# Edge groups of eight tiles in two slots, with sums and one-hot rows in two places

## The chip, the cores and the metric

One core of one Trainium2 chip. The time is the device time of one execution in microseconds; the kernel before has three of them, 4353.99, 4359.96 and 4360.02 us (median 4359.96).

## The reference, cut to what matters

The program is a chain of four graph layers over 3125 nodes with 128 features and 100000 edges that are sorted by destination. The change lies in the last layer, which sends a message along every edge:

```python
m_in = jnp.concatenate([h[src], h[dst], edge_attr], axis=1)
msg = jax.nn.relu(m_in @ msg_w1 + msg_b1) @ msg_w2 + msg_b2
agg = jax.ops.segment_sum(msg, dst, num_segments=h.shape[0])
```

## The kernel before, in words

Nodes are held in 25 blocks of 125 (`B`), edges in tiles of 128. Because matmul and sum commute, the edge stage computes only the relu and its sum by destination; `msg_w2` is applied in `update_phase`. `message_table_phase` has prepared two tables: h @ (the source half of `msg_w1`) in HBM (`dr.table`), and h @ (the destination half) plus bias in SBUF as three bf16 parts (`a3.q_parts`).

`edge_phase` (line 2019) takes the edges in groups of `GT` = 4 tiles, 196 groups in 49 rounds of `SLOTS` = 4 slots. For a group in slot s:

- SyncE (L2060, L2061) loads the destinations of its 512 edges, broadcast over 125 partitions (`dst_row`), and the edge attribute with its parts (`ea_row`).
- POOL (L2076) gathers the source rows by four indirect DMAs, one per tile, into `rows[s]`. It waits for `s_pre[s]`, that is for the identity matmul of the group that had the slot before (L2073).
- VectorE `turned` (L2102) compares `dst_row` with the lane numbers of a block: `hot_t[s]`, a one-hot matrix, 125 lanes by 512 edges.
- PE `inputs` puts the input of the relu together in one PSUM bank per slot: edge attribute (L2152, 4 matmuls), destination rows `hot_t` x `q_parts` (L2160, 12 matmuls, 3 for each tile), and the gathered rows by an identity matmul of 512 columns (L2167), which counts up `s_pre[s]`. An fp32 matmul shows as two rows of the trace, a bf16 one as one.
- ScalarE (L2204) applies relu to the bank's 512 columns and writes `act[s]`.
- VectorE `sums` first adds the sum of the visit before from its PSUM bank to `agg_t` (L2093), then makes `hot[s]` (L2111), one-hot rows with edges on partitions. PE `sums` (L2179) multiplies `act` and `hot`, 4 fp32 matmuls, into the one bank `SUMS`.

A group whose edges lie in more than one block is visited once for each block (`blocks.each`, L2009): the steps of L2102, L2160, L2093, L2111 and L2179 are repeated. The list of each group's first and last block, `g.groups`, is made in `setup_phase` (L300 to L314) from the smallest and largest destination of its tiles.

The order is written out by hand. PE and VectorE do `inputs` or `turned` of the next group, then `sums` of this one (`round_of`, L2185, L2118). POOL and SyncE run ahead, up to four groups, held by `s_pre` alone.

Of the kernel before, what the change touches and what calls it, by code (L numbers as in the profile page):

```python
# [16 lines left out]
B = 125  # L17
# [23 lines left out]
SLOTS = 4  # L41
# [83 lines left out]
def setup_phase(nc, g, io):  # L125

    with Phase(nc, "setup") as ph:
# [16 lines left out]
        NGR = NT // 4  # L144
# [94 lines left out]
        def _(v):  # L239
# [60 lines left out]
            for k, (i, op) in enumerate(((1, ALU.min), (0, ALU.max))):  # L300
                last = v.tensor_reduce(gm[:, k, :], mxb[0:1, i, :].rearrange("a (n t) -> a n t", t=4), AX.X, op)
# [445 lines left out]
def program(nc, io, out):  # L747
    ctx = ExitStack()
    Phase.used.clear()
    with ctx:  # L750
# [15 lines left out]
        g.groups = sb("groups", [1, NT // 4], I32)  # L766
# [1252 lines left out]
def edge_phase(nc, g, dr, a3):  # L2019
# [3 lines left out]
    GT = 4  # L2023
    W = GT * 128
    ROUNDS = (E // 128 + 1 + GT * SLOTS - 1) // (GT * SLOTS)
    with Phase(nc, "edge") as ph:
        rows = [ph.sb(f"rows{s}", [128, GT, D]) for s in range(SLOTS)]
        act = [ph.sb(f"act{s}", [128, GT, D]) for s in range(SLOTS)]
        hot = [ph.sb(f"hot{s}", [128, GT, B]) for s in range(SLOTS)]
# [4 lines left out]
        lane = ph.sb("lane", [128, 1])  # L2034
        ps = ph.ps()
        s_lane = ph.sem("lane")
        s_rows = [ph.sem(f"rows{s}") for s in range(SLOTS)]
# [11 lines left out]
        SUMS = SLOTS  # L2049

        @block.sync
        def _(sp):
            dst = dr.dst_rows.rearrange("(r s k) -> r s k", s=SLOTS, k=W)
            ea = dr.ea_rows.rearrange("i (r s k) -> i r s k", s=SLOTS, k=W)
            with sp.Fori(0, ROUNDS) as r:
                for s in range(SLOTS):

                    sp.wait_ge(s_pre[s], sp.snap(r + 1))
                    sp.sem_inc(s_tick, 1)
                    sp.dma_start(dst_row[s][:], dst[bass.ds(r, 1), s, :].to_broadcast([B, W])).then_inc(s_dst[s], 16)  # L2060
                    sp.dma_start(ea_row[s][:], ea[:, bass.ds(r, 1), s, :].rearrange("i a k -> i (a k)")  # L2061
                                 ).then_inc(s_ea[s], 16)

        @block.gpsimd
        def _(pool):
            pool.iota(lane_id[:], [[1, B]], base=0, channel_multiplier=0,
                      allow_small_or_imprecise_dtypes=True).then_inc(s_lane, 1)
            pool.iota(lane[:], [[0, 1]], base=0, channel_multiplier=1,
                      allow_small_or_imprecise_dtypes=True).then_inc(s_lane, 1)
            for r in range(ROUNDS):  # L2070
                for s in range(SLOTS):

                    pool.wait_ge(s_pre[s], r + 1)  # L2073
                    for i in range(GT):
                        t = (r * SLOTS + s) * GT + i
                        pool.indirect_dma_start(rows[s][:, i, :], None, dr.table,  # L2076
                                                bass.IndirectOffsetOnAxis(ap=g.src_idx[:, t:t + 1], axis=0)
                                                ).then_inc(s_rows[s], 16)

        @block.vector  # L2080
        def _(v):
# [5 lines left out]

            def add_sums(n):

                v.wait_ge(s_sum, n)  # L2090
                v.wait_ge(s_added, n)
                at = a3.agg_t[:, bass.ds(v.snap(before, min_val=0, max_val=NB - 1) * B, B)]
                v.tensor_tensor(at, at, ps[:, SUMS, 0:B], ALU.add).then_inc(s_added, 1)  # L2093

# [12 lines left out]
            def sums(r, s):  # L2107
                def one(d):
                    add_sums(added.next())
                    v.reg_mov(before, d)  # L2110
                    v.scalar_tensor_tensor(hot[s][:], bc(g.dst[:, bass.ds(r * (SLOTS * GT) + s * GT, GT)], B),  # L2111
                                           g.block_base[:, bass.ds(d, 1)],
                                           lane_id[:].unsqueeze(1).to_broadcast([128, GT, B]),
                                           ALU.add, ALU.is_equal).then_inc(s_hot, 1)

# [21 lines left out]
        def _(pe):  # L2137
# [3 lines left out]
            pe.sem_inc(s_sum, 1)  # L2141
            for s in range(SLOTS):
                pe.sem_inc(s_free[s], 1)
                pe.sem_inc(s_pre[s], 1)
                pe.sem_inc(s_act[s], 1)

            def inputs(r, s, ahead):

                pe.wait_ge(s_act[s], r + 1)
                pe.wait_ge(s_ea[s], r * 16 + 16)  # L2150
                for i in range(GT):
                    pe.matmul(ps[:, s, i * 128:(i + 1) * 128], ea_row[s][:, i * 128:(i + 1) * 128], a3.w_parts[:],  # L2152
                              start=i == 0, stop=False, skip_group_check=True)

                def one(d):
                    n = used[s].next()
                    pe.wait_ge(s_hot_t[s], n)
                    for i in range(GT):
                        for p in range(3):
                            last = pe.matmul(ps[:, s, i * 128:(i + 1) * 128], hot_t[s][:, i * 128:(i + 1) * 128],  # L2160
# [5 lines left out]
                pe.wait_ge(s_rows[s], r * (16 * GT) + 16 * GT)  # L2166
                pe.matmul(ps[:, s, :], g.ident[:], rows[s][:].rearrange("p a k -> p (a k)"), start=False, stop=True,  # L2167
                          skip_group_check=True).then_inc(s_pre[s], 1)

            def sums(r, s):  # L2170

                pe.wait_ge(s_act[s], r + 2)

                def one(d):
                    n = summed.next()

                    pe.wait_ge(s_hot, n)
# [14 lines left out]

            inputs(0, 0, False)
# [195 lines left out]
```

## Time and profile before

| what | value |
|---|---|
| median of three runs | 4359.96 us |
| the profiled execution: its own time | 4348.9 us |
| its span | 4347.1 us |
| PE busy | 3458.5 us, 80% |
| VectorE (DVE) busy | 1530.1 us, 35% |
| ScalarE (ACT) busy | 1228.8 us, 28% |
| POOL busy | 818.1 us, 19% |
| mean granted clock of PE over the span | 0.898 |

The span is the time from the first to the last instruction. A line of the timeline gives the start in us from the span's start, how long the instruction (or the merged run of instructions, with its count) takes, engine, line, operation, and in brackets how long the engine was idle before it and what ended that. "issue" means that the profile shows nothing that it waited for, "remote" that the semaphore moved at a time at which no row of its writer ends. Matmul ends are modelled. PEld are PE's weight loads. SPq are the DMAs that SyncE issues. A granted clock of 1.00 is 2.4 GHz, of 0.50 is 1.2 GHz.

### The profile page before, as it was taken

How to read it: one execution, taken by the hardware profiler on the slowest of the kernel's cores; microseconds unless marked ns; L12 is line 12 of the kernel's file. 1: busy time of each engine (PE TensorE's matmuls, PEld its weight loads, DVE VectorE, ACT ScalarE, POOL GpSimd, SP SyncE). 2: the span in 40 equal slices, each digit the busy share in tenths (PEclk: the TensorE clock that was granted, in tenths of full speed). 3: DMA queues.
4: the chain of work that ended last, by engine and by line, in shares of the span. 5: the costliest groups of instructions: out<-in, count | busy, mean ns of one | idle time of the engine just before them, and what ended most of it. 6: DMA issues, size and time to landing. Idle time of an engine off the chain costs nothing. (4 is left out here: it accounts for less than half of the span.)

```text
span 4347.1 us, 81151 instructions
## 1 busy us (share of the span) xinstructions
PE 3458.5 (80%) x23430; PEld 2425.0 (56%) x23431; DVE 1530.1 (35%) x4257; ACT 1228.8 (28%) x3843; POOL 818.1 (19%) x839
## 2 busy tenths in 40 slices
PE   2887778888988989897899999995665666666666
PEld 1334445566764444343799999994444444445454
DVE  8766556666760210002441111123222222222223
ACT  1455556677860210002432221212000000000000
POOL 3100000000000000000000000001666565656552
PEclk7999999999999999997999999997777777777777
DMA  2001111223349378993343222251222222222221
GB/s 58 0 29 44 58 58 58 87 88 102 102 134 237 92 184 188 204 210 88 80 124 88 74 80 73 67 145 35 66 65 64 60 64 57 63 61 63 59 59 40
DMA packets 120584, 381.40 MB, mean 88 GB/s; under 512 B 32903, under 2 KB 75262, under 8 KB 106556
## 3 DMA queue, kind: packets, MB, share of 16 engines
q1 hardware_dynamic: 95090, 326.87, 28.2%
q0 software_dynamic: 25216, 51.44, 5.4%
q8 instruction: 99, 1.62, 0.2%
q14 instruction: 179, 1.47, 0.1%
HBM read 294.59 MB, written 83.62 MB: 87 GB/s over the span
## 5 line engine op out<-in xcount | busy, mean ns | idle before, releaser
L2076 POOL DMA_INDIRECT edge_rows<-src_table,src_idx x784 | 759.5, 969 | 501.8 <-issue 195.3
L571 ACT ACTIVATE build_scaled<-build_lanes,w 128x128 f32<-128x128 bf16 x1132 | 440.2, 404 | 496.1 <-DVE build_lanes L529 468.9
L2179 PE MATMUL edge_ps<-edge_hot,edge_act 128*128 128x125 f32 x1760 | 305.9, 329 | 312.1 <-DVE edge_hot L2111 241.7
L2179 PEld LDWEIGHTS edge_ps<-edge_hot,edge_act 128*128 128x128 f32 x1760 | 288.6, 239 | 467.3 <-DVE edge_hot L2111 305.4
L529 DVE TENSOR_SCALAR build_lanes<-key_id,lane,one_w 128x128 f32<-128x128 f16 x1132 | 402.7, 356 | 382.3 <-PE build_ps L642 284.3
L642 PE MATMUL build_ps<-build_keys,build_scaled 128*128 128x300 bf16 (+1 forms) x2264 | 504.0, 305 | 29.0 <-ACT build_scaled L571 24.4
L634 PE MATMUL build_ps<-build_keys,build_lanes 128*128 128x300 bf16 (+1 forms) x1132 | 350.6, 310 | 170.3 <-DVE build_keys L531 149.2
L1041 PE MATMUL prop_ps<-prop_rows,y 125*128 125x500 f32 (+1 forms) x1050 | 413.6, 552 | 52.3 <-DMA prop_rows<-adj_rows 45.4
L2204 ACT ACTIVATE edge_act<-edge_ps 128x512 f32<-128x512 f32 x196 | 117.1, 597 | 1159.9 <-remote 654.7
L531 DVE TENSOR_SCALAR build_keys<-key_id,key,win_base 128x300 bf16<-128x300 f16 (+1 forms) x1132 | 423.7, 374 | 0.8
L1263 POOL TENSOR_SCALAR qk_half_b<-a_wob 125x128 f32<-125x128 f32 x1 | 2.1, 2061 | 1894.0 <-DMA a_wob<-L_gnn_Wo_b_dram 1894.0
L638 PE MATMUL build_ps<-build_keys,build_lanes 128*128 128x300 bf16 (+1 forms) x1132 | 344.3, 304 | 0.0
L1041 PEld LDWEIGHTS prop_ps<-prop_rows,y 125*128 125x128 f32 x1050 | 190.1, 193 | 274.6 <-issue 199.3
L2160 PE MATMUL edge_ps<-m_q_parts,edge_hot_t 125*128 x2640 | 243.3, 255 | 124.8 <-DVE edge_hot_t L2102 67.9
L2093 DVE TENSOR_TENSOR m_agg_t<-m_agg_t,edge_ps 128x125 f32 x221 | 63.0, 285 | 729.8 <-remote 469.9
L634 PEld LDWEIGHTS build_ps<-build_keys,build_lanes 128*128 128x128 bf16 x1132 | 111.0, 98 | 345.9 <-DVE build_keys L531 321.0
L642 PEld LDWEIGHTS build_ps<-build_keys,build_scaled 128*128 128x128 bf16 x2264 | 188.5, 100 | 180.0 <-ACT build_scaled L571 87.5
L2160 PEld LDWEIGHTS edge_ps<-m_q_parts,edge_hot_t 125*128 125x128 bf16 x2640 | 194.8, 115 | 160.2 <-issue 145.4
L2167 PE MATMUL edge_ps<-edge_rows,ident 128*128 128x512 f32 x392 | 267.2, 769 | 5.6 <-issue 3.5
L1565 PE MATMUL orders_ps<-a_xp,n 125*125 125x256 bf16 (+2 forms) x3000 | 262.4, 249 | 0.0
L1565 PEld LDWEIGHTS orders_ps<-a_xp,n 125*125 125x125 bf16 x3000 | 258.9, 139 | 0.6 <-issue 0.4
L1565 PE MATMUL orders_ps<-a_xp,orders_panel 125*125 125x256 bf16 (+2 forms) x3000 | 259.0, 247 | 0.0
(386 smaller groups left out, 4331.0 us busy)
## 6 DMA issues: line engine op xcount, KB each, us to landing
prop_rows<-adj_rows SPq DMA_DIRECT2D x85, 1367.2 KB
cnt_panels<-build_cnt SPq DMA_DIRECT2D x50, 683.6 KB
adj_rows<-build_adj_t SPq DMA_DIRECT2D x25, 1367.2 KB
n<-cnt_panels SPq DMA_DIRECT2D x40, 683.6 KB
orders_panel<-cnt_panels SPq DMA_DIRECT2D x40, 683.6 KB
edge_dst_row<-dst_rows SPq DMA_DIRECT2D x196, 125.0 KB
h<-cnt_panels SPq DMA_DIRECT2D x20, 683.6 KB
prop_rows<-adj_rows SPq DMA_DIRECT2D x85, 158.7 KB
```

What stands on the lines that cost most here:

```text
L529: v.tensor_scalar(lanes[s][:], g.key_id[:, 0:128], g.lane[:, at], g.one_w3[:, at], ALU.is_equal, ALU.mult).then_inc(s_lanes[s], 1)
L531: v.tensor_scalar(keys[s][:, 0:KW[q] + q], g.key_id[:, 0:KW[q] + q], g.key[:, at], g.win_base[:, q, bass.ds(e, 1)], ALU.subtract, ALU.is_e ...
L571: a.activation(scaled[s][:], half(lanes[s], 1), ACT.Copy, scale=g.w12[:, bass.ds(t, 1)]).then_inc(s_scaled[s], 1)
L634: done = pe.matmul(ps[:, count_bank(j, parity), 0:KW[j % 2]], half(lanes[s], 1), keys[s][:, 0:KW[j % 2]], start=first, stop=False, skip_gr ...
L638: pe.matmul(ps[:, weight_bank(j), 0:KW[j % 2]], half(lanes[s], 0), keys[s][:, 0:KW[j % 2]], start=first, stop=False, skip_group_check=True)
L642: last = pe.matmul(ps[:, weight_bank(j), 0:KW[j % 2]], half(scaled[s], i), keys[s][:, 0:KW[j % 2]], start=False, stop=False, skip_group_ch ...
L1041: last = pe.matmul(ps[:, c, 0:n * B], (y[0:B] if h else g.h)[:, row, 0:D], rows[row % R][:, b0 * B:(b0 + n) * B], start=at == 0, stop=at = ...
L1565: last = pe.matmul(ps[0:B, bank, at.start:hi], panel[i][:, b * B:(b + 1) * B], x_in[k][:, b, p, at.start:hi], start=False, stop=b == NB - ...
L2076: pool.indirect_dma_start(rows[s][:, i, :], None, dr.table, bass.IndirectOffsetOnAxis(ap=g.src_idx[:, t:t + 1], axis=0)).then_inc(s_rows[s ...
L2160: last = pe.matmul(ps[:, s, i * 128:(i + 1) * 128], hot_t[s][:, i * 128:(i + 1) * 128], a3.q_parts[:, bass.ds(d, 1), p, :].rearrange("p a ...
L2167: pe.matmul(ps[:, s, :], g.ident[:], rows[s][:].rearrange("p a k -> p (a k)"), start=False, stop=True, skip_group_check=True).then_inc(s_p ...
L2179: last = pe.matmul(ps[:, SUMS, 0:B], act[s][:, i, :], hot[s][:, i, :], start=i == 0, stop=i == GT - 1)
```

## The change

Groups have eight tiles (`GT` = 8) and there are two slots: 98 groups in 49 rounds. `g.groups` and the reductions that make it have half the entries. A slot owns two PSUM banks, one for each half of four tiles (`bank`); the two banks of the sums are 4 and 5, taken in turn (`side`), and `hot` too has two places by parity. Identity matmul, relu and the wait of the gathers go by halves: `s_pre` and `s_act` count up twice per group, `s_rows` is one semaphore for each half. VectorE makes the hot rows of a visit before it adds the sum of the one before. PE waits for `s_added` ahead of a sum. PE also gets matmuls whose result nobody reads (`keep_on`): zeros of 512 columns into bank 7, three ahead of the gathered rows of each group and two ahead of its sums.

```diff
-SLOTS = 4
+SLOTS = 2
...
-        NGR = NT // 4
+        NGR = NT // 8
...
-    GT = 4
+    GT = 8
+    HT = GT // 2
...
-        hot = [ph.sb(f"hot{s}", [128, GT, B]) for s in range(SLOTS)]
+        hot = ph.sb("hot", [128, 2, GT * B])
...
+        still = ph.sb("still", [128, HT * 128], BF16)
...
-        SUMS = SLOTS
+        SUMS, IDLE = 2 * SLOTS, 7
+
+        def bank(s, i):
+
+            return ps[:, 2 * s + i // HT, i % HT * 128:(i % HT + 1) * 128]
+
+        def half_of(tile, i):
+            return tile[:, HT * i:HT * i + HT, :].rearrange("p a k -> p (a k)")
...
-                    sp.wait_ge(s_pre[s], sp.snap(r + 1))
+                    sp.wait_ge(s_pre[s], sp.snap(r * 2 + 1))
...
+            pool.memset(still[:], 0.0).then_inc(s_still, 1)
...
-
-                    pool.wait_ge(s_pre[s], r + 1)
                     for i in range(GT):
+                        if i % HT == 0:
+                            pool.wait_ge(s_pre[s], 2 * r + 1 + i // HT)
...
-                                                ).then_inc(s_rows[s], 16)
+                                                ).then_inc(s_rows[s][i // HT], 16)
...
+            def side(n):
+                return v.snap(n & 1, min_val=0, max_val=1)
+
             def add_sums(n):
 
-                v.wait_ge(s_sum, n)
+                v.wait_ge(s_sum, n + 1)
                 v.wait_ge(s_added, n)
...
             def sums(r, s):
                 def one(d):
-                    add_sums(added.next())
-                    v.reg_mov(before, d)
-                    v.scalar_tensor_tensor(hot[s][:], bc(g.dst[:, bass.ds(r * (SLOTS * GT) + s * GT, GT)], B),
+                    n = added.next()
+
+                    v.wait_ge(s_sum, n)
+                    v.scalar_tensor_tensor(hot[:, bass.ds(side(n), 1), :].rearrange("p a (t k) -> p (a t) k", k=B), bc(g.dst[:, bass.ds(r * (SLOTS * GT) + s * GT, GT)], B),
                                            g.block_base[:, bass.ds(d, 1)],
                                            lane_id[:].unsqueeze(1).to_broadcast([128, GT, B]),
                                            ALU.add, ALU.is_equal).then_inc(s_hot, 1)
+                    add_sums(n)
+                    v.reg_mov(before, d)
...
+            def keep_on(n):
+
+                for i in range(n):
+                    pe.matmul(ps[:, IDLE, :], still[:, 0:128], still[:], start=True, stop=True, skip_group_check=True)
...
-                pe.wait_ge(s_rows[s], r * (16 * GT) + 16 * GT)
-                pe.matmul(ps[:, s, :], g.ident[:], rows[s][:].rearrange("p a k -> p (a k)"), start=False, stop=True,
-                          skip_group_check=True).then_inc(s_pre[s], 1)
+                keep_on(3)
+                for i in range(2):
+                    pe.wait_ge(s_rows[s][i], r * (16 * HT) + 16 * HT)
+                    pe.matmul(ps[:, 2 * s + i, :], g.ident[:], half_of(rows[s], i), start=False, stop=True,
+                              skip_group_check=True).then_inc(s_pre[s], 1)
 
             def sums(r, s):
 
-                pe.wait_ge(s_act[s], r + 2)
+                keep_on(2)
+                pe.wait_ge(s_act[s], r * 2 + 4)
 
                 def one(d):
                     n = summed.next()
-
+                    here = pe.snap(n & 1, min_val=0, max_val=1)
+                    sums_bank = ps[:, bass.ds(here + SUMS, 1), 0:B].rearrange("p a k -> p (a k)")
                     pe.wait_ge(s_hot, n)
+
+                    pe.wait_ge(s_added, n)
                     for i in range(GT):
-                        last = pe.matmul(ps[:, SUMS, 0:B], act[s][:, i, :], hot[s][:, i, :], start=i == 0,
-                                         stop=i == GT - 1)
+                        last = pe.matmul(sums_bank, act[s][:, i, :],
+                                         hot[:, bass.ds(here, 1), i * B:(i + 1) * B].rearrange("p a k -> p (a k)"),
+                                         start=i == 0, stop=i == GT - 1)
...
-                    a.wait_ge(s_pre[s], a.snap(r + 2))
-                    a.activation(act[s][:].rearrange("p a k -> p (a k)"), ps[:, s, :], ACT.Relu).then_inc(s_act[s], 1)
+                    for i in range(2):
+                        a.wait_ge(s_pre[s], a.snap(r * 2 + 3 + i))
+                        a.activation(half_of(act[s], i), ps[:, 2 * s + i, :], ACT.Relu).then_inc(s_act[s], 1)
```

## Rows read from the trace of the kernel before

**Rows 1.** The page: busy time by engine, and the gathers among the costliest groups.
```profile
PE 3458.5 (80%) x23430; PEld 2425.0 (56%) x23431; DVE 1530.1 (35%) x4257; ACT 1228.8 (28%) x3843; POOL 818.1 (19%) x839
...
L2076 POOL DMA_INDIRECT edge_rows<-src_table,src_idx x784 | 759.5, 969 | 501.8 <-issue 195.3
```

**Rows 2.** The timeline of the stage's first run of gathers (POOL, PE, ACT).
```profile
3014.45 1.09 POOL L2076 DMA_INDIRECT edge_rows<-src_table,src_idx  x1 [1.59 <-PEq L2143]
...
3033.04 0.27 PE L2160 MATMUL edge_ps<-m_q_parts,edge_hot_t 125*128 x1 [1.90 <-issue]
...
3035.88 0.26 PE L2160 MATMUL edge_ps<-m_q_parts,edge_hot_t 125*128 x1 [2.57 <-issue]
...
3038.52 0.95 POOL L2076 DMA_INDIRECT edge_rows<-src_table,src_idx  x1 [0.30 <-issue]
...
3043.06 0.60 ACT L2204 ACTIVATE edge_act<-edge_ps 128x512 f32<-128x512 f32 x1 [14.41 <-remote]
```

**Rows 3.** The timeline at the end of the stage.
```profile
4273.19 0.94 POOL L2076 DMA_INDIRECT edge_rows<-src_table,src_idx  x1 [0.30 <-issue]
...
4287.48 0.60 ACT L2204 ACTIVATE edge_act<-edge_ps 128x512 f32<-128x512 f32 x1 [2.31 <-PE edge_ps L2167]
...
4290.79 0.29 DVE L2093 TENSOR_TENSOR m_agg_t<-m_agg_t,edge_ps 128x125 f32 x1 [1.37 <-PE edge_ps L2179]
```

**Rows 4.** Windows over the stage: PE, PEld, DVE, ACT, POOL busy, granted clock, DMA share, GB/s.
```profile
3013.00:4289.00 1276.00, 825.35 (x5568) 601.08 (x5568) 300.40 (x662) 117.06 (x196) 759.46 (x784) 0.77 0.25 61
```

**Rows 5.** Groups of the stage by line: count, busy us, mean ns, idle before.
```profile
L2179 PE MATMUL edge_ps<-edge_hot,edge_act 128*128 128x125 f32 x1752 | 304.7, 329 | 310.9 <-DVE edge_hot L2111 240.5 <-issue 70.1
...
L2160 PE MATMUL edge_ps<-m_q_parts,edge_hot_t 125*128 x2640 | 243.3, 255 | 124.8 <-DVE edge_hot_t L2102 67.9 <-issue 55.8
...
L2111 DVE SCALAR_TENSOR_TENSOR edge_hot<-dst,block_base,edge_lane_id 128x500 f32<-128x500 f32 x220 | 161.2, 733 | 0.3 <-issue 0.3
```

**Rows 6.** The timeline of a run of four gathers and the run of eight behind it.
```profile
3546.03 0.95 POOL L2076 DMA_INDIRECT edge_rows<-src_table,src_idx  x1 [1.30 <-PE edge_ps L2167]
...
3548.41 1.08 PE L2167 MATMUL edge_ps<-edge_rows,ident 128*128 128x512 f32 x2
...
3551.81 0.60 ACT L2204 ACTIVATE edge_act<-edge_ps 128x512 f32<-128x512 f32 x1 [5.42 <-remote]
...
3552.05 0.95 POOL L2076 DMA_INDIRECT edge_rows<-src_table,src_idx  x1 [1.32 <-remote]
...
3553.02 1.16 PE L2179 MATMUL edge_ps<-edge_hot,edge_act 128*128 128x125 f32 x8 [0.64 <-DVE edge_hot L2111]
...
3554.43 0.84 PE L2160 MATMUL edge_ps<-m_q_parts,edge_hot_t 125*128 x12
...
3555.11 1.08 PE L2167 MATMUL edge_ps<-edge_rows,ident 128*128 128x512 f32 x2
...
3563.88 0.60 ACT L2204 ACTIVATE edge_act<-edge_ps 128x512 f32<-128x512 f32 x1 [6.76 <-remote]
...
3564.11 1.44 POOL L2076 DMA_INDIRECT edge_rows<-src_table,src_idx  x1 [2.37 <-remote]
```

**Rows 7.** The timeline where PE has half its clock, and around a two-block group.
```profile
3612.52 1.46 PE L2160 MATMUL edge_ps<-m_q_parts,edge_hot_t 125*128 x12
...
3613.77 2.02 PE L2167 MATMUL edge_ps<-edge_rows,ident 128*128 128x512 f32 x2
...
3624.47 0.95 POOL L2076 DMA_INDIRECT edge_rows<-src_table,src_idx  x1 [1.38 <-remote]
...
3640.18 0.95 POOL L2076 DMA_INDIRECT edge_rows<-src_table,src_idx  x1 [5.95 <-PE edge_ps L2167]
```

**Rows 8.** Waits of POOL in the stage: us in total, times, longest us.
```profile
POOL edge_rows L2076 <- PE edge_ps L2167: 166.1, 60, 7.6
POOL edge_rows L2076 <- remote: 138.8, 88, 3.8
```

**Rows 9.** Groups of POOL over the span, shapes kept apart: its widest clear.
```profile
L189 POOL MEMSET setup_raw<- 128x896 f32 x1 | 0.8, 846 | 0.0
```

More of the change, by code:

```diff
@@ L300, in _ @@
             for k, (i, op) in enumerate(((1, ALU.min), (0, ALU.max))):
-                last = v.tensor_reduce(gm[:, k, :], mxb[0:1, i, :].rearrange("a (n t) -> a n t", t=4), AX.X, op)
+                last = v.tensor_reduce(gm[:, k, :], mxb[0:1, i, :].rearrange("a (n t) -> a n t", t=8), AX.X, op)
             do(last)
@@ L765, in program @@
         g.block_base = sb("block_base", [128, NB])
-        g.groups = sb("groups", [1, NT // 4], I32)
+        g.groups = sb("groups", [1, NT // 8], I32)
         g.spans = sb("spans", [1, 260], I32)
@@ L2034, in edge_phase @@
         lane = ph.sb("lane", [128, 1])
+        still = ph.sb("still", [128, HT * 128], BF16)
         ps = ph.ps()
         s_lane = ph.sem("lane")
-        s_rows = [ph.sem(f"rows{s}") for s in range(SLOTS)]
+        s_still = ph.sem("still")
+        s_rows = [[ph.sem(f"rows{s}_{i}") for i in range(2)] for s in range(SLOTS)]
         s_dst = [ph.sem(f"dst{s}") for s in range(SLOTS)]
@@ L2086, in _ @@
             v.reg_mov(before, 0)
+            def side(n):
+                return v.snap(n & 1, min_val=0, max_val=1)
             def add_sums(n):
-                v.wait_ge(s_sum, n)
+                v.wait_ge(s_sum, n + 1)
                 v.wait_ge(s_added, n)
                 at = a3.agg_t[:, bass.ds(v.snap(before, min_val=0, max_val=NB - 1) * B, B)]
-                v.tensor_tensor(at, at, ps[:, SUMS, 0:B], ALU.add).then_inc(s_added, 1)
+                v.tensor_tensor(at, at, ps[:, bass.ds(side(n + 1) + SUMS, 1), 0:B].rearrange("p a k -> p (a k)"),
+                                ALU.add).then_inc(s_added, 1)
             def turned(r, s, ahead):
@@ L2140, in _ @@
             summed = Counter(pe)
-            pe.sem_inc(s_sum, 1)
+            pe.sem_inc(s_sum, 2)
             for s in range(SLOTS):
                 pe.sem_inc(s_free[s], 1)
-                pe.sem_inc(s_pre[s], 1)
-                pe.sem_inc(s_act[s], 1)
+                pe.sem_inc(s_pre[s], 2)
+                pe.sem_inc(s_act[s], 2)
+            def keep_on(n):
+                for i in range(n):
+                    pe.matmul(ps[:, IDLE, :], still[:, 0:128], still[:], start=True, stop=True, skip_group_check=True)
             def inputs(r, s, ahead):
-                pe.wait_ge(s_act[s], r + 1)
+                pe.wait_ge(s_act[s], r * 2 + 2)
                 pe.wait_ge(s_ea[s], r * 16 + 16)
                 for i in range(GT):
-                    pe.matmul(ps[:, s, i * 128:(i + 1) * 128], ea_row[s][:, i * 128:(i + 1) * 128], a3.w_parts[:],
-                              start=i == 0, stop=False, skip_group_check=True)
+                    pe.matmul(bank(s, i), ea_row[s][:, i * 128:(i + 1) * 128], a3.w_parts[:],
+                              start=i % HT == 0, stop=False, skip_group_check=True)
                 def one(d):
@@ L2159, in one @@
                         for p in range(3):
-                            last = pe.matmul(ps[:, s, i * 128:(i + 1) * 128], hot_t[s][:, i * 128:(i + 1) * 128],
+                            last = pe.matmul(bank(s, i), hot_t[s][:, i * 128:(i + 1) * 128],
                                              a3.q_parts[:, bass.ds(d, 1), p, :].rearrange("p a k -> p (a k)"),
@@ L2191, in round_of @@
                     sums(r, s)
+            pe.wait_ge(s_still, 1)
             inputs(0, 0, False)
```

## The prediction

> **What bounds the kernel now.** I read the page first: TensorE (PE) is busy for 80% of the span, but line 2076, the gathers on POOL, is a stage of its own in the last third, with 759.5 us of busy time [rows 1]. Ahead of that stage the change touches only the size of a few short reductions. The stage runs from the first gather at 3014.45 [rows 2] to the last addition at 4290.79 [rows 3]: 1276 us of a span of 4347.1. In it PE is busy 825 us and POOL 759 us, and the mean granted clock is 0.77 [rows 4]. No engine is full, so I looked at who waits.
>
> The code has 49 rounds of four slots, 196 groups of four tiles; VectorE makes 220 one-hot tiles (L2111 x220 [rows 5]), so 24 groups lie over two blocks. Of one group's rows on PE, the products take 0.84 us, the identity matmul 1.08 and the sums 1.16 at full clock [rows 6], the first two 1.46 and 2.02 at half (1.2 GHz) [rows 7]. With the last gather behind them, the last groups follow each other in 2.91 us: the relu at 4287.48 came 2.31 us after the end of the one before and lasts 0.60 [rows 3]. Over the stage a group takes 1276/196 = 6.5 us. So gathers, or what goes with them, more than double its price.
>
> POOL's wait rows say how: apart from its own gaps of 0.30 us, which make a rhythm of 1.25 us per gather [rows 2], it waits 148 times (60 and 88), 304.9 us together, for a PE result [rows 8]. Alone it would need 784 x 1.25 = 980 us.
>
> **The rows that decide.** Take a run of four gathers from 3546.03. PE's identity matmul has its row at 3548.41 and lasts 1.08 us, yet ScalarE's relu, which waits for it alone, starts at 3551.81, and POOL goes on at 3552.05 [rows 6]. From the start of the run to the release: 5.78 us, 1.45 per gather. Then a run of eight from 3552.05: the identity matmul with its row at 3555.11 releases the relu at 3563.88, 11.83 us after the start, 1.48 per gather [rows 6]. The first run, of twenty, starts at 3014.45, its last gather at 3038.52, and its release is at 3043.06: 28.61 us, 1.43 per gather; late in it PE's matmul rows come one by one, 2.8 us apart (3033.04, 3035.88) [rows 2]. Three lengths, one law: **while gathers are issued back to back, PE's results come through late, mostly about 1.45 us per gather after the run began**; PE runs ahead for a while and then crawls. I call this the hold. The rows show it; they don't show its cause.
>
> The Trainium skill (TensorE: Matmul & The Clock Gate, on engine queue depths) gives PE a queue of 64 instructions. PE's rows running ahead and then thinning out agree with that; no number below rests on it.
>
> So the stage is a chain: run of gathers, hold, release, next run. 784 x 1.45 = 1137 us of the 1276 are hold, the rest is what PE, VectorE and POOL need after a release.
>
> **The change, part by part.** (a) *Visits.* Boundaries stay 24, groups become 98: 122 visits of eight tiles, 976 tile visits for 880. PE's visit work (L2160 243.3 us, L2179 304.7 [rows 5]) grows by 96/880, 60 us of busy time, on the path only where PE is late, below. (b) *VectorE* is busy 300 us in the stage [rows 4]. The same columns plus 11%, in 122 steps of each kind for 220: nothing, covered by POOL and PE; without that cover it costs what it costs today. (c) *Sums and hot rows in two places.* Now VectorE adds the last sum and only then makes the hot rows: from the release (3551.81) to PE's next sums (3553.02) pass 1.2 us [rows 6]. With two places the hot rows lie ready: 1.2 us less after each release. PE's new wait for s_added needs the addition before last, a group old by then: nothing. But VectorE's wait for s_sum still stands ahead of the next wide compare (`turned`) in its queue, and PE's products wait for that compare; at nothing if the sum is in time, the compare's 0.8 us plus the sum's delay if not (rival C). (d) *Halves.* Identity matmul, relu and gathers stay at four tiles, so 16 tiles stay in flight; relu 0.60 us as now. (e) *Idle matmuls.* Five of 512 bf16 columns per group, 490 in all. No row has this form. From the rows of 12 matmuls (0.84 and 1.46 us, less 0.22 and 0.22 for the last, over 11: 0.056 and 0.113 for 128 columns [rows 6, 7]) one costs 0.22 to 0.45 us; three stand just ahead of the identity matmul. (f) *POOL's clear* of `still` ahead of the first gather: nothing to the 0.85 us of a clear of 896 columns [rows 9]; I take 0.6. SyncE's 392 issues become 196 of twice the bytes, a group ahead as before: nothing.
>
> (g) *The run of gathers* is the term that matters. PE now does both halves' identity matmuls one after the other, so POOL is released for eight gathers at once and nearly every run is of eight: a hold of 8 x 1.45 = 11.6 us, then 0.24 until POOL restarts (3551.81 to 3552.05). What does PE get through in such a run? Between the releases at 3551.81 and 3563.88 [rows 6] it completes two identity steps with their inputs and one block of sums: 18 + 8 + 18 = 44 matmul rows. The new group needs 2 + 2 idle + 16 + 8 + 24 + 3 idle + 2 = 57 from one release to the next. Thirteen are over: eight of 0.056, three idle of 0.22, one identity step of 1.08, 2.2 us at full clock. Bounds: 0 (all pass) and 6.0 (24 products, three idle, identity, all after the release at half clock). I take 2.2, from the run of eight that is nearest, less the 1.2 of (c): 1.0.
>
> So a group of eight takes 11.6 + 0.24 + 1.0 = 12.85 us, where a run of four now takes 6.02 (3546.03 to 3552.05) and of eight 12.06 (3552.05 to 3564.11) [rows 6]. A second block costs a further compare, products and release: the run of eight that holds one starts at 3624.47, the next run at 3640.18 [rows 7], 15.7 us against 12.06: about 4 us, 24 times, 96 us (bounds 1 and 6 each).
>
> **Sum.** The first twenty gathers take 28.9 us as now; 764 are left, 95.5 groups x 12.85 = 1227; + 96 + 28.9 + 17 (end of the last gathers to the last addition) + 3 for the wider last group + 0.6 = 1372 us for 1276: +96. The profiled execution took 4348.9 us, so 4445. The median of the runs, 4359.96, lies 11 us above it. About 0.2% is what a measurement can tell from nothing here.
>
> **Rivals.** *A, the run of eight suffices (faster).* All 57 rows pass in the hold, and the second places hide the second blocks: 95.5 x 11.85 = 1132, + 49 for both ends as above = 1181 with second blocks hidden, -95, **4254**. For it: 12.06 us for eight tiles is already seen, and PE's waits for hot rows (240.5 us [rows 5]) go. Against: 13 more rows in the same hold. Its mechanism gains if idle matmuls lift the clock from the mean of 0.77 [rows 4].
> The Trainium skill (same page, HAM oscillation) says that waits between bursts of matmuls bring the clock down; the mean of 0.77 agrees, and by that rule the idle matmuls help and the time would be A's.
> *B, the hold is no law of the gathers* but comes from the add-then-compare chain that the change cuts: then POOL's rhythm is the bound, 980 + 20 = 1000 us, -276, **4073**. Against: three run lengths agree, and in the run of twenty PE crawls in mid-block, where no such chain can be. *C, slower still:* the sums of a group don't complete before the hold sets in, VectorE's compare stays stuck behind them, and all inputs follow the release: 11.85 + 6.0 = 17.85, for some two thirds of the groups (the others catch the start of a run): 15.9 x 95.5 + 96 + 49 = 1663, +387, **4736**. *D, nothing changes:* about 12.3 us per eight tiles as now, 4350 to 4370.
>
> **Chances.** Forecast 0.50 (its own range 4375 to 4590), A 0.28 (4180 to 4350), B 0.10, C 0.09, D 0.03. The range 4180 to 4590 leaves out B and C. Faster: B and most of A, 0.36; slower: forecast and C, 0.59; within 0.2%: D and the edge of A, 0.05.
>
> **What would show it.** In the changed trace POOL's waits number near 100 for 148 but last over 2.5 us; a relu starts 11.6 us or more after a run of eight begins and the next run some 1 us later than that; L2160's products x2928, the sums x1952; granted clock over 0.77. If POOL's mean wait is below 2 us, or runs over eight are common, A holds; if nearly all its gaps are 0.30 us, B; if products follow each release in a block and POOL waits 4 us and more, C. I am wrong in kind if the stage is under 1276 us.

## The result, and the profile after

| | before | after |
|---|---|---|
| median of 4 runs beside each other | 4356.98 us (4351.37 to 4360.02) | 4429.43 us (4415.73 to 4440.94) |
| ratio, 95% interval | | 1.0167 (1.0129 to 1.0204) |
| profiled execution, its span | 4348.9, 4347.1 us | 4420.44, 4418.6 us |
| first gather to last addition | 3014.45 to 4291.1: 1276.6 us | 3004.62 to 4362.2: 1357.6 us |
| mean granted clock in that stage | 0.77 | 0.81 |

The change costs 1.7%, 72 us; the forecast of 4445 lies 16 us above the measurement. It was counted up from the profiled execution (4348.9 us); as a step it said +96 us, and +72 was measured. The stage grew by 81 us. In this execution it began 10 us earlier; over the eleven traces of this study that have gathers the first one lies between 2996.0 and 3015.2 us, after a part that none of the experiments touches, so lengths of the stage tell more than single totals. Times and ratios leave out slow executions, those over 1.5% above the fastest of the same kernel; of all runs told of here that is one, 8555.86 us of the kernel with one clear.

The page of the changed kernel: instructions of each engine, and the groups that answer to [rows 1, 5]. The gathers are L2088 now, the relu L2237, the products L2184, the sums L2209, the identity matmul L2193.

```profile
PE 3594.0 (81%) x24350; PEld 2499.7 (57%) x24401; DVE 1484.4 (34%) x3963; ACT 1221.9 (28%) x3843; POOL 824.5 (19%) x840
...
L2088 POOL DMA_INDIRECT edge_rows<-src_table,src_idx x784 | 765.8, 977 | 577.4 <-PE edge_ps L2193 261.2
...
L2184 PE MATMUL edge_ps<-m_q_parts,edge_hot_t 125*128 x2928 | 268.9, 254 | 220.7 <-DVE edge_hot_t L2118 120.8
...
L2209 PE MATMUL edge_ps<-edge_hot,edge_act 128*128 x1952 | 296.3, 303 | 91.2 <-issue 90.8
...
L2193 PE MATMUL edge_ps<-edge_rows,ident 128*128 128x512 f32 x392 | 232.0, 696 | 23.7 <-issue 21.0
```

The wait rows of POOL, answering to [rows 8] (what for: us in total, times, the longest):

```profile
POOL edge_rows L2088 <- PE edge_ps L2193: 261.2, 43, 9.2
...
POOL edge_rows L2088 <- remote: 103.4, 52, 2.9
```

95 waits for 148, as forecast, but 3.8 us each: 364.6 us for 304.9. They are of two kinds, with longest waits of 9.2 and 2.9 us.

The wait that the second places were meant for did go. Put down to the hot rows, PE stood idle for 240.5 us before [rows 5]; now it is 0.4 us ahead of the sums, and 4.1 ahead of the idle matmuls in front of them:

```profile
L2209 PE MATMUL edge_ps<-edge_hot,edge_act 128*128 x1952 | 296.3, 303 | 91.2 <-issue 90.8 <-DVE edge_hot L2128 0.4
```

The wait for the wide compare rose instead, from 67.9 [rows 5] to 120.8 us (L2184), and the stage got longer. Idle time of PE inside a hold was not what the stage was waiting for.

The next two stretches of the timeline show one of each kind of POOL's waits (start, duration, engine, line; idle time before in brackets). First a group of eight that lies in one block:

```profile
3740.17 0.94 POOL L2088 DMA_INDIRECT edge_rows<-src_table,src_idx  x1 [7.90 <-PE edge_ps L2193]
...
3743.31 0.28 DVE L2108 TENSOR_TENSOR m_agg_t<-m_agg_t,edge_ps  x1 [4.20 <-PE edge_ps L2209]
3743.45 1.51 PE L2184 MATMUL edge_ps<-m_q_parts,edge_hot_t 125*128 x24
...
3748.97 0.94 POOL L2088 DMA_INDIRECT edge_rows<-src_table,src_idx  x1 [0.30 <-issue]
3750.18 0.37 PE L2209 MATMUL edge_ps<-edge_hot,edge_act 128*128 x1 [0.95 <-issue]
...
3751.87 1.08 ACT L2237 ACTIVATE edge_act<-edge_ps 128x512 f32<-128x512 f32 x2 [10.48 <-remote]
...
3752.10 0.94 POOL L2088 DMA_INDIRECT edge_rows<-src_table,src_idx  x1 [2.19 <-remote]
```

The run of eight starts at 3740.17, the relu comes 11.70 us later, POOL goes on at 3752.10: 11.93 us, which is hold and restart and nothing else. The sum of the group before is added 3.1 us into the run. Of the 93 runs of eight (before the last) half are followed by the next within 12.04 us, 5% within 11.88. Next, a group over two blocks:

```profile
3722.59 0.94 POOL L2088 DMA_INDIRECT edge_rows<-src_table,src_idx  x1 [2.27 <-PE edge_ps L2193]
...
3725.15 1.68 PE L2184 MATMUL edge_ps<-m_q_parts,edge_hot_t 125*128 x24
...
3731.33 0.94 POOL L2088 DMA_INDIRECT edge_rows<-src_table,src_idx  x1 [0.30 <-issue]
3734.32 0.55 DVE L2118 TENSOR_SCALAR edge_hot_t<-edge_dst_row,block_base,edge_lane 125x1024 bf16<-125x1024 int16 x1 [16.62 <-remote]
3735.01 2.77 PE L2184 MATMUL edge_ps<-m_q_parts,edge_hot_t 125*128 x24 [8.17 <-DVE edge_hot_t L2118]
...
3737.57 1.47 PE L2169 MATMUL edge_ps<-edge_still 128*128 128x512 bf16 x3
...
3738.85 1.90 PE L2193 MATMUL edge_ps<-edge_rows,ident 128*128 128x512 f32 x4
3739.93 0.60 ACT L2237 ACTIVATE edge_act<-edge_ps 128x512 f32<-128x512 f32 x1 [16.50 <-PE edge_ps L2193]
...
3740.17 0.94 POOL L2088 DMA_INDIRECT edge_rows<-src_table,src_idx  x1 [7.90 <-PE edge_ps L2193]
```

The first block's 24 products have their row at 3725.15, but VectorE's compare for the second block, which waits for them (s_free), starts at 3734.32: 11.73 us after the run began, the hold again. Only then come 24 products (2.77 us), three idle matmuls (1.47) and the identity matmul. POOL goes on 17.58 us after the run began, 5.65 more than above.

Now the stage can be counted. From the first gather to the start of the last run (4336.73) pass 1332.1 us for 97 groups: 97 x 11.95 = 1159, and 173 are left for 24 second blocks, 7.2 each. The same count for the kernel before, with 6.02 us per group of four [rows 6]: 1255 us to the start of its last run, 195 x 6.02 = 1174, 81 left, 3.4 each. So by this count the change gave back 0.09 us per plain group of eight (9 us) and lost 3.8 us on each of 24 second blocks (91). The split hangs on the 6.02, which comes from one run of eight; the groups of four with no second block near them take 6.08 us in the mean, and with that it is 0.21 given back and 4.3 lost (2.9 for 7.2). The trace also shows the price without a subtraction: from the first gather of one group to the first of the next pass 17.81 us in the mean where PE has a second block to do in between (24 times), 11.97 in the median elsewhere (72). That is 5.8 of the 7.2; the rest falls on groups behind.

### The profile page after: what moved, and what is told of

Its sections match the earlier page's. It is cut to its first block and busy times, and to the rows that moved or that the text cites. A ratio compares the mean times of both kernels' runs of the same rounds, so it can differ in the third digit from the quotient of the medians.

```text
span 4418.6 us, 80967 instructions
## 1 busy us (share of the span) xinstructions
PE 3594.0 (81%) x24350; PEld 2499.7 (57%) x24401; DVE 1484.4 (34%) x3963; ACT 1221.9 (28%) x3843; POOL 824.5 (19%) x840
## 3 DMA queue, kind: packets, MB, share of 16 engines
q0 software_dynamic: 25216, 51.44, 5.3%
## 5 line engine op out<-in xcount | busy, mean ns | idle before, releaser
L2088 POOL DMA_INDIRECT edge_rows<-src_table,src_idx x784 | 765.8, 977 | 577.4 <-PE edge_ps L2193 261.2
L2237 ACT ACTIVATE edge_act<-edge_ps 128x512 f32<-128x512 f32 x196 | 110.9, 596 | 1245.9 <-PE edge_ps L2193 664.9
L2184 PE MATMUL edge_ps<-m_q_parts,edge_hot_t 125*128 x2928 | 268.9, 254 | 220.7 <-DVE edge_hot_t L2118 120.8
L2209 PE MATMUL edge_ps<-edge_hot,edge_act 128*128 x1952 | 296.3, 303 | 91.2 <-issue 90.8
L2184 PEld LDWEIGHTS edge_ps<-m_q_parts,edge_hot_t 125*128 125x128 bf16 x2928 | 219.2, 115 | 259.8 <-issue 250.1
L2209 PEld LDWEIGHTS edge_ps<-edge_hot,edge_act 128*128 128x128 f32 x1952 | 277.7, 216 | 139.0 <-issue 129.6
L1565 PEld LDWEIGHTS orders_ps<-a_xp,orders_panel 125*125 125x125 bf16 x3000 | 255.5, 137 | 0.0
L2193 PE MATMUL edge_ps<-edge_rows,ident 128*128 128x512 f32 x392 | 232.0, 696 | 23.7 <-issue 21.0
```

Source lines behind the costliest of these rows:

```text
L1565: last = pe.matmul(ps[0:B, bank, at.start:hi], panel[i][:, b * B:(b + 1) * B], x_in[k][:, b, p, at.start:hi], start=False, stop=b == NB - ...
L2088: pool.indirect_dma_start(rows[s][:, i, :], None, dr.table, bass.IndirectOffsetOnAxis(ap=g.src_idx[:, t:t + 1], axis=0)).then_inc(s_rows[s ...
L2184: last = pe.matmul(bank(s, i), hot_t[s][:, i * 128:(i + 1) * 128], a3.q_parts[:, bass.ds(d, 1), p, :].rearrange("p a k -> p (a k)"), start ...
L2193: pe.matmul(ps[:, 2 * s + i, :], g.ident[:], half_of(rows[s], i), start=False, stop=True, skip_group_check=True).then_inc(s_pre[s], 1)
L2209: last = pe.matmul(sums_bank, act[s][:, i, :], hot[:, bass.ds(here, 1), i * B:(i + 1) * B].rearrange("p a k -> p (a k)"), start=i == 0, st ...
```

## The experiments

Every kernel ran beside the kernel before on the same chip; its median there was 4344.6 to 4353.4 us, except for the last experiment.

**What makes the hold.** Three kernels fetch the source rows otherwise; none gives every edge its own source row, and the stage's other work is untouched.

```diff
-  pool.indirect_dma_start(rows[s][:, i, :], None, dr.table, ...src_idx[:, t:t + 1]...)
+  sp.dma_start(rows[s][:, i, :], dr.table[u:u + 128, :])        # plain_sync: in SyncE's loop
+  pool.dma_start(rows[s][:, i, :], dr.table[u:u + 128, :])      # plain_pool: in place of the gather
+  pool.indirect_dma_start(rows[s][0:64, i, :], ..., src_idx[0:64, t:t + 1]...)   # half_gather
```

> The changed kernel with the gathers left out: the same bytes come as plain copies of 128 rows of the table each, issued by SyncE, so the edges get wrong source rows. If POOL's issue of gathers is what holds PE's results, the hold is gone, each semaphore comes at the end of its matmul, and a group of eight is bound by PE's own work, 972 / 98 = 9.9 us at the clock seen and about 6.5 at full clock, plus waits: 7 to 9 us a group, total 3700 to 3900. Rival: the hold comes from rows landing in SBUF while PE works, whoever asks for them: then about 11 us or more a group and a total above 4200.

> The changed kernel with the gathers left out, as in the run with plain copies by SyncE (wrong source rows), but the plain copies of 128 rows each are issued by POOL, one where a gather was. If it is the indirect gather that holds PE's results, the hold is gone here too and the total is near that run's 3833 us (3800 to 3950). If any transfer that POOL issues does it, the total stays above 4200, with a release some fixed time per copy after a run's start.

> The changed kernel with half of each gather left out: each fetches 64 rows for 128, the other half of the tile stays zero, so half the edges get no source row. If the hold is a price per gather, a run of eight still holds PE's results to 11.7 us and the total stays within 30 us of 4429. If it is a price per row, which POOL runs ahead of, the hold is about half (5.9 us, or POOL's own issue if that is longer), POOL or PE becomes the bound at 7 to 10 us a group, and the total is 3850 to 4200.

Measured (one run each): 3832.96, 3843.73 and 4426.79 us. The windows rows of the stage, of plain_sync and then of half_gather (busy us of each engine, granted clock, DMA share, GB/s):

```profile
3009.00:3775.00 766.00, 730.17 (x6496) 559.41 (x6544) 251.78 (x367) 117.21 (x196) 0.00 (x0) 1.00 0.34 101
```

```profile
3015.00:4368.00 1353.00, 968.82 (x6546) 667.02 (x6546) 256.77 (x367) 111.18 (x196) 736.21 (x785) 0.82 0.15 39
```

Without gathers the stage takes 770 us from the first copy to the last addition, for 1358 with the same bytes moved; over the window above PE is busy for 95% of the time and its clock is full. With plain copies issued by POOL it is nearly the same (772 us), and they go through the queue that the gathers use, 51.44 MB in 25216 packets in both kernels; so neither POOL's queue nor the landing of rows does it. With half the rows per gather the hold stays, although half the bytes move (25.75 MB, in as many packets). Here is one run of eight of that kernel, release 11.61 us after its start.

```profile
3061.55 0.91 POOL L2091 DMA_INDIRECT edge_rows<-src_table,src_idx  x1 [2.23 <-remote]
...
3070.34 0.91 POOL L2091 DMA_INDIRECT edge_rows<-src_table,src_idx  x1 [0.30 <-issue]
3073.16 1.09 ACT L2240 ACTIVATE edge_act<-edge_ps 128x512 f32<-128x512 f32 x2 [10.75 <-remote]
```

The semaphore events say the same: in both plain kernels all 196 identity results arrive 0.01 to 0.02 us after the modelled end of the matmul, in the changed kernel 111 of 196 arrive over 1 us late. The hold is a price per indirect gather that POOL issues, not per row. What inside the chip collects it stays open. Three things are not told apart: that the rows are scattered (the plain copies read the same few stretches of the table over and over), that they are looked up through an index, and POOL's own work on each (0.94 us for a gather, 0.91 for half a one, 0.54 for a plain copy). Nor do the rows say whether a held matmul is late itself or only the news of its end, since matmul ends are modelled.

**What the change is worth without the hold.** The kernel before, its gathers replaced by the same plain copies from SyncE.

> The kernel before with the gathers left out in the same way (plain copies of 128 rows of the table issued by SyncE, wrong source rows for the edges). With the hold gone this tells what the change's other parts are worth: the changed kernel so altered took 3833 us. If the second places matter when nothing is held (1.2 us per group of four on the chain from add to compare), the kernel before is slower by tens of us up to 200: 3870 to 4030. Rival: PE alone is the bound in both, and the kernel before, with 96 tile visits less and no idle matmuls, is faster: 3760 to 3830.

```profile
3007.00:3709.00 702.00, 640.37 (x5576) 481.49 (x5576) 296.64 (x661) 117.02 (x196) 0.00 (x0) 0.99 0.38 111
```

3767.36 us: the rival held. At full clock the change makes the stage longer by 64 us (702 to 766 in the windows), PE's busy time grows by 90. The idle matmuls alone would explain that. Three of them, from plain_sync, and what follows:

```profile
3300.78 0.81 PE L2165 MATMUL edge_ps<-edge_still 128*128 128x512 bf16 x3
3301.43 1.88 PE L2189 MATMUL edge_ps<-edge_rows,ident 128*128 128x512 f32 x4
```

One row is 0.38 us long but overlaps the next; by their starts they cost 0.65 / 3 = 0.22 us each, 490 of them 106 us. The second places do return something here: PE's idle time for hot rows goes from 28.6 us to nothing. It doesn't pay for the idle matmuls, and the wait for the compare takes half of it back (17.2 to 31.7 us).

**Letting the results through in mid-run.** Three, two and one clears by POOL ahead of the fifth gather of each run.

```diff
+  if i == HT:
+      for k in range(3):        # pause; 2: pause_two_clears; 1: pause_one_clear
+          pool.memset(pause[:], 0.0).then_inc(s_pause, 1)      # 128x896 bf16
+          pool.wait_ge(s_pause, (r * SLOTS + s) * 3 + k + 1)
```

> The changed kernel with three POOL clears of 896 columns (0.85 us each, about 2.6 us together) between the fourth and the fifth gather of each run. My theory: it is the back-to-back issue of gathers that holds PE's results; they come through about 1 us after POOL stops issuing, so in the middle of the run already. POOL then seldom waits, a group takes about 8 x 1.25 + 2.9 = 12.9 us, second blocks cost 0 to 1: the stage is about 98 x 12.9 = 1265 to 1300 us for 1357, total 4330 to 4365. Rival 1: any POOL work holds them, or they come by a fixed time after the run's end: a plain group takes 11.95 + 2.9 = 14.8 us, total about 4700. Rival 2: the hold counts gathers but the pause is too short: the same as rival 1.

> As the kernel with three clears in mid-run, with two (about 1.8 us). POOL then stops issuing 4.7 us after a run's start and goes on at about 6.5. My theory: PE's results come 5.8 us after the start of four gathers (1.45 us each, while POOL issues one per 1.25), so they still get through; a group takes 8 x 1.25 + 1.9 = 11.9 us, second blocks stay as cheap as with three clears: about 75 us less than with three, total 4270 to 4295. Rival: the pause is too short, what gets through is a part, and second blocks cost again what they cost without a pause: 4430 or more.

> As above with one clear (0.85 us and its wait). POOL goes on at about 5.7 us after a run's start, just before PE's results are due at 5.8. My theory: they don't get through, the hold goes on to the end of the run and is longer by the pause at most: 11.95 to 12.9 us a group and second blocks at 6 us: total 4430 to 4520. Rival: any stop of POOL's issue lets PE's results through at once: a group takes 8 x 1.25 + 1.0 = 11.0 us and the total is 4180 to 4230.

| | us | ratio to before (95%) | stage | POOL's waits for PE results |
|---|---|---|---|---|
| changed kernel | 4429.43 | 1.0167 (1.0129 to 1.0204) | 1357.6 | 364.6 us in 95 |
| pause (three) | 4356.18 | 1.0015 (0.9998 to 1.0033) | 1296.7 | 7.4 us in 9 |
| two clears | 4317.11 | 0.9934 (0.9904 to 0.9964) | 1249.7 | 51.5 in 23 |
| one clear | 4360.41 | 1.0028 (1.0000 to 1.0056) | 1305.8 | 244.0 in 88 |

POOL's wait row for PE's results in the kernel with three clears:

```profile
POOL edge_rows L2094 <- PE edge_ps L2199: 7.4, 9, 1.4
```

It works as the hold predicts: a stop that outlasts the 5.8 us of four gathers frees the results, and idle time of 2.94 us per group, 2.64 more than the usual gap, wins 61 us of stage. POOL's own pace becomes the bound, eight gathers and the pause: runs of eight follow each other in 12.64 us at the least. From one group's first gather to the next one's pass 13.58 us in the mean where a second block lies in between (24), 13.00 elsewhere (72): 0.6 us are left of the 5.8. With two clears (a stop of 2.03 us) runs of eight take 11.74 us at the least and 12.17 in the mean, and by the same count a second block still costs 2.1 us (14.19 against 12.14); the forecast of 4270 to 4295 had the sign and not the size. One clear stops POOL for 1.13 us, so it goes on 5.82 us after the run's start, and the other half's run then ends in a wait: 5.82 + 6.18 = 12.0 us for a plain group, about as without a pause. From the first gather to the start of the last group pass 1281.6 us; less 97 x 12.0 that leaves 4.9 us for each second block, where it was 7.2. So even this stop lets a part through, which neither side of the expectation had: 4360 lies 70 below the theory's 4430 and 130 above the rival's 4230.

**The second block's price, taken apart.** One kernel without the idle matmuls, one with hot_t in two places so that the second compare needs no PE result.

```diff
-                keep_on(3)          # no_idle
-                keep_on(2)
...
-        hot_t = [ph.sb(f"hot_t{s}", [B, W], BF16) for s in range(SLOTS)]        # early_compare
+        hot_t = [ph.sb(f"hot_t{s}", [B, 2, W], BF16) for s in range(SLOTS)]
-                pe.sem_inc(s_free[s], 1)
+                pe.sem_inc(s_free[s], 2)
```

> The changed kernel without its idle matmuls. My theory: a group in one block takes 11.95 us because PE's results are held to the end of a run of eight gathers, and five idle matmuls fit inside that; so these groups stay at 11.95 us. In a group over two blocks three idle matmuls stand behind the hold, 0.49 us each: 24 x 1.5 = 36 us less, total about 4390 to 4400. Rival: the idle matmuls are what keeps the clock at 0.81 over the stage; without them it falls to 0.77 or below, the work behind the hold gets longer, and the total is 4430 or more.

> The changed kernel with the wide one-hot rows (hot_t) in two places by parity, so that the compare for a second block no longer waits for the first block's products. My theory: a second block costs some 6 us because VectorE's second compare waits for s_free, a PE result that is held to the end of the run, and the compare, 24 products and the rest then follow the hold. With the compare made early the cost falls to about 1 us: 24 x 5 to 6 = 120 to 144 us less, total 4285 to 4310. Rival: the second block's 24 products don't pass the hold even when their input lies ready (24 more rows in it), and 3 us or more remain: 4350 or more.

| | us | ratio (95%) | stage | first gather to last run's start, less 97 x 11.95, per second block |
|---|---|---|---|---|
| no_idle | 4382.69 | 1.0080 (1.0055 to 1.0106) | 1333.8 | 6.2 us |
| early_compare | 4396.96 | 1.0103 (1.0070 to 1.0136) | 1332.4 | 6.1 us |

The matmul rows of the stage of no_idle (x instructions, busy us, mean ns, idle before), beside those of the changed kernel above:

```profile
L2207 PE MATMUL edge_ps<-edge_hot,edge_act 128*128 x1952 | 342.9, 321 | 150.5 <-issue 149.2
L2184 PE MATMUL edge_ps<-m_q_parts,edge_hot_t 125*128 x2928 | 285.1, 268 | 230.1 <-DVE edge_hot_t L2118 132.4 <-issue 97.3
L2192 PE MATMUL edge_ps<-edge_rows,ident 128*128 128x512 f32 x392 | 264.4, 807 | 5.6 <-issue 4.5 <-DMA edge_rows<-src_table,src_idx 0.7
```

The idle matmuls do keep the clock: without them the stage runs at 0.74 for 0.81, and an identity matmul takes 807 ns for 696. The stage is shorter all the same, by 24 us, and 4382.69 lies below the 4390 to 4400 that was expected: slower matmuls inside the hold cost nothing that shows, idle ones behind it 0.43 us each (1.28 us for three, 3737.57 to 3738.85 in the changed kernel, at half clock). The rule of the Trainium skill (TensorE: Matmul & The Clock Gate, HAM oscillation), that waits between bursts bring the clock down, agrees with 0.74 against 0.81; the time went the other way. The early compare was worth 25 us, not 120 to 144: its rival came out. A run of eight of early_compare with a second block in it:

```profile
3719.79 0.95 POOL L2088 DMA_INDIRECT edge_rows<-src_table,src_idx  x1 [2.33 <-remote]
...
3723.26 1.95 PE L2185 MATMUL edge_ps<-m_q_parts,edge_hot_t 125*128 x30
...
3729.25 0.95 POOL L2088 DMA_INDIRECT edge_rows<-src_table,src_idx  x1 [0.30 <-issue]
3729.88 0.28 PE L2185 MATMUL edge_ps<-m_q_parts,edge_hot_t 125*128 x1 [1.18 <-issue]
3731.30 1.23 PE L2185 MATMUL edge_ps<-m_q_parts,edge_hot_t 125*128 x10 [1.14 <-issue]
...
3735.78 0.95 POOL L2088 DMA_INDIRECT edge_rows<-src_table,src_idx  x1 [5.58 <-PE edge_ps L2194]
```

The compare no longer stands in the way: the first 30 products follow each other without a gap, where the changed kernel stopped after 24. But the second block's 24 products are 24 more rows in the hold. From the 31st on they come one or two at a time, and ten are left when the last gather is through (3730.20). POOL goes on 15.99 us after the run began, for 17.58 in the changed kernel.

**One part alone.** Sums and hot rows in two places, in the kernel before.

```diff
-        hot = [ph.sb(f"hot{s}", [128, GT, B]) for s in range(SLOTS)]
+        hot = ph.sb("hot", [128, 2, GT * B])
...
-                v.wait_ge(s_sum, n)
+                v.wait_ge(s_sum, n + 1)
...
-                    add_sums(added.next())
-                    v.reg_mov(before, d)
                     v.scalar_tensor_tensor(hot[...], ...)
+                    add_sums(n)
+                    v.reg_mov(before, d)
```

> The kernel before with one part of the change alone: sums and hot rows in two places by parity, still groups of four tiles and four slots. I forecast 1.2 us less after each release for it. By what the changed kernel shows, a plain group is bound by the hold: a run of four takes 5.8 us and its restart 0.24, and the runs of four last 6.13 us in the median, so at most 0.1 us each goes, with a little from second blocks: 4335 to 4355. Rival: the 1.2 us is on the path of every release that POOL waits for (148): 4180 or so.

4328.36 us, ratio 0.9944 (0.9918 to 0.9971), 16 us less than the kernel before and a little below its forecast. Its profiled execution, at 4346.99 us the slowest of its ten, shows a stage of 1276.2 us, as before (1276.6), and POOL still waits 153 times; so 180 us are excluded, and where the 0.6% comes from that trace doesn't show.

**Versions that might beat both.** First the edits of pause_two_clears, no_idle and early_compare together, as one kernel:

> The changed kernel with three edits together: two clears as a pause in the middle of each run, no idle matmuls, and the wide one-hot rows in two places. My theory: what costs in the changed kernel is only what stands behind the hold in groups over two blocks; the pause alone gave 4317. Without the idle matmuls and with the early compare the remaining long groups shrink, and the floor is 98 x 11.75 + 46 = 1198 us of stage against 1249.7 in the run with the pause alone: total 4275 to 4305, faster than both kernels. Rival: without the idle matmuls the clock falls (0.74 for 0.82 over the stage) and takes that back: 4310 to 4350.

4273.87 us, ratio 0.9828 (0.9792 to 0.9863), faster than both kernels, and 1 us below its forecast of 4275 to 4305. POOL's waits for PE in it, the clear's own wait, and the windows row of its stage:

```profile
POOL edge_rows L2094 <- POOL edge_pause L2091: 26.6, 98, 0.3
POOL edge_rows L2094 <- PE edge_ps L2199: 1.7, 2, 1.0
```

```profile
3011.00:4222.00 1211.00, 862.86 (x6056) 634.03 (x6056) 262.87 (x367) 111.48 (x196) 957.49 (x980) 0.81 0.25 65
```

Two waits of 1.7 us together: POOL is the bound, busy for 957 of 1211 us, with 208 us of its own gaps and 27 of waits for its clears beside that. The clock stayed at 0.81 though the idle matmuls went.

The second puts the pause alone into the kernel before:

```diff
                 for s in range(SLOTS):                 # before_pause: the kernel before, four slots
+                    if s % 2 == 1:
+                        ... two clears, as above ...
                     pool.wait_ge(s_pre[s], r + 1)
```

> The kernel before with nothing but the pause: two POOL clears of 896 columns (about 1.8 us) ahead of every second group's four gathers (odd slots). My theory: PE's results come 5.8 us after the start of a run of four, POOL stops at 4.7 and goes on at 6.5, so its waits for PE go, eight tiles take 8 x 1.25 + 1.9 = 11.9 us where they take 12.1 to 12.2 now, and second blocks, some 3 us each now (24), cost next to nothing: 98 x 11.9 + 46 = 1212 us of stage for 1277, total 4275 to 4300. Then the mend needs no group of eight. Rival: with groups of four the releases already lie between the runs (98 runs of four), and the pause adds to POOL's waits rather than taking their place: 4345 or more.

This run doesn't answer its question, and shows more than was asked. It ran on another chip, and there the kernel before took 4074.37 us (4058.73 to 4082.41 in 9 runs), 6% less than on the three chips of the other experiments; with the pause it took 4228.85, ratio 1.0376 (1.0354 to 1.0399). Its timeline has no hold:

```profile
3542.09 1.04 POOL L2081 DMA_INDIRECT edge_rows<-src_table,src_idx  x1 [0.27 <-POOL edge_pause L2076]
...
3548.46 2.07 PE L2172 MATMUL edge_ps<-edge_rows,ident 128*128 128x512 f32 x2 [3.72 <-DMA edge_rows<-src_table,src_idx]
3549.68 0.94 POOL L2081 DMA_INDIRECT edge_rows<-src_table,src_idx  x1 [0.30 <-issue]
3550.57 0.60 ACT L2209 ACTIVATE edge_act<-edge_ps 128x512 f32<-128x512 f32 x1 [7.19 <-PE edge_ps L2172]
3550.93 0.94 POOL L2081 DMA_INDIRECT edge_rows<-src_table,src_idx  x1 [0.30 <-issue]
3551.87 1.76 POOL L2076 MEMSET edge_pause<- 128x896 bf16 x2
...
3553.90 0.95 POOL L2081 DMA_INDIRECT edge_rows<-src_table,src_idx  x1 [0.27 <-POOL edge_pause L2076]
```

The identity matmul (two rows) ends at 3550.53, the relu follows at 3550.57, in the middle of a run of gathers; by the semaphore events none of the 196 identity results is over 1 us late. POOL never waits for one. Where nothing is held the pause is lost time. It makes the gap between two gathers 2.03 us (3551.87 to 3553.90) for 0.30, 98 x 1.73 = 170 us in all. The medians differ by 154.5, and 1177.7 us of stage less 154.5 makes 1023 for the kernel before on that chip, near the 1000 that rival B gave for POOL alone. That 1023 is an estimate: the kernel before was timed on that chip and not traced there. The changed kernel never ran there, so what the change is worth with gathers and without a hold isn't known. Whether the pause helps the kernel before where there is a hold was not tried either.

## Why the prediction was right

The bound was read rightly: run of gathers, hold, release, next run. That the sum came within 16 us was in part luck: two terms missed by 87 and by 77 us, in opposite senses. The sign that a plain group would end 1 us after the hold didn't come out either.

- *The hold, 11.6 + 0.24.* Measured 11.70 and 0.23. Its condition, gathers issued back to back, is now shown by taking them away. That it is a law of the gathers holds on the chips used first, and not on the last one.
- *The remainder of 1.0 us in a plain group of eight* was about 0.1: all 57 rows pass where 44 were seen, as rival A said. 97 groups x 0.9: the forecast had 87 us too much. The forecast for second places, below, was part of this sum. What failed is the step "thirteen are over": the 44 rows completed in a run before were what PE was given to do, not what it could do.
- *Second blocks, about 4 us each,* were 7.2: 77 us too little. The price was carried over from a run of eight of the kernel before, where a second block has 12 products and no idle matmuls. Now 24 products, the wide compare and 1.3 us of idle matmuls follow the hold. Bounds of 1 and 6 were too narrow; with three clears in the run a second block costs 0.6 us (13.58 against 13.00), since results come in the pause.
- *Second places, 1.2 us per release:* alone in the kernel before they were worth 16 us, 0.17 us per eight tiles; in the changed kernel plain groups gained 0.09 to 0.21 us by all parts together. The hold covers the chain from addition to compare. Rival C is out: the sum is in time (the addition at 3743.31). So is rival D: the ratio lies between 1.0129 and 1.0204.
- *Visits, +60 us of PE's busy time:* products and sums together 548.0 to 565.2 us, +17 and not +60. The sums' rows got shorter (303 ns for 329) while the clock was 0.81 for 0.77; without gathers, at full clock, both kernels show them at 275 and 276 ns. *Idle matmuls, 0.22 to 0.45 us each:* right, 0.22 at full clock and 0.43 at half. *POOL's clear, 0.6:* 0.52.
- *Rival A* came out for plain groups and not for second blocks; its claim that a higher clock carries the kernel there is refuted by no_idle. *Rival B* is what the times of the kernel before look like on the last chip.

## What to carry to other kernels

When an engine's results come late behind a stream of another engine's instructions, count how many such waits stand one behind the other in a step; a dependence that crosses the engines twice (products, compare, products) pays outside the cover, and doubling the tile doubled what stands there (2.9 to 3.4 us, then 7.2, of which the idle matmuls were about 1). A wait of 240 us that a change removes is worth little if it lay under another one. A price taken from a row with half the work is a lower bound, not a middle. Try a short stop in the stream before rebuilding the tiling: two clears took the changed kernel from 1.0167 to 0.9934 of the time before. And try it on more than one chip, since where nothing is held it costs what it lasts.

## What the hardware showed that was not expected

- Indirect gathers issued back to back by POOL hold PE's completions for 1.45 us each (5.8 us for four, 11.7 for eight); plain copies issued by POOL don't (772 us of stage for 1358), and gathers of 64 rows hold like those of 128 (11.61 us for eight).
- One chip of those used doesn't do it: 4074 us for the same kernel that takes 4345 to 4357 on the others, and a relu 0.04 us after its matmul in mid-run. What sets that chip apart isn't known.
- The stage's granted clock and PE's busy time didn't go together: 0.81 with 972 us of work in 1358, 0.81 with 863 in 1211 and no idle matmuls, 0.74 with 922 in 1334.
